# Attention A in 64-column matmuls with a new order of its batch, and one read moved in attention B

## What is computed

```python
# attention A: 16 heads of 8, R = 8 value groups, on a normalised x
xn = _ln(x, g1, b1)
q = _lin(xn, Wq, bq).reshape(b, n, H, HD) / np.sqrt(HD)
k = _lin(xn, Wk, bk).reshape(b, n, H, HD)
score = softmax(einsum('bihd,bjhd->bhij', q, k), axis=-1)
v = _lin(xn, Wv, bv).reshape(b, n, R, HD)
out = einsum('bhij,bjrd->bihrd', score, v)
comp = softmax(concatenate([qv, out], axis=-1) @ Ws.T + bs, axis=3)
out = (comp * out).sum(axis=3).reshape(b, n, DIM)
...
# the program
x = x + attn_a(_layernorm(x))      # attn_a: the above, then a dense block with its own norm
x = x + ffn(_layernorm(x))         # two matrices without an activation between: folded into one
x = x + attn_b(_layernorm(x))      # attention with a memory, segments of 64 tokens
x = x + ffn(_layernorm(x))
```

## Time and profile before

| | us |
|---|---|
| median of 3 runs | 1479.66 (1475.42 to 1479.83) |
| the profiled execution | 1480.59 |
| its span, first to last instruction | 1478.7 |

### The profile page before, as it was taken

How to read it: one execution, slowest core, us unless ns; L and a number is a source line. 1 busy time by engine, 2 the same in 40 slices (tenths; PEclk the granted TensorE clock), 3 DMA queues, 4 the chain that set the end, 5 groups by cost and what they waited for, 6 DMA issues and landing times. The chain is left out here.

```text
span 1478.7 us, 53395 instructions
## 1 busy us (share of the span) xinstructions
PE 1279.3 (87%) x17796; PEld 1160.4 (78%) x17796; DVE 1014.3 (69%) x2754; ACT 886.4 (60%) x2084; POOL 874.4 (59%) x1167
## 2 busy tenths in 40 slices
PE   5999999999999999999984877648989898888896
PEld 4799898998898999899973666427878778777785
DVE  3558778778778788788762444346777777777764
ACT  2456666666676676666652666445665656565653
POOL 3546676676676776667644888564444444444441
PEclk9899999999999999999995999869999999999998
DMA  5443332332332332322303444135454444454541
GB/s 145 122 130 95 83 107 64 95 99 71 96 89 80 97 89 81 96 78 79 97 8 114 122 129 128 43 106 140 144 141 136 145 137 147 137 147 138 147 137 42
DMA packets 181703, 158.26 MB, mean 107 GB/s; under 512 B 12529, under 2 KB 163185, under 8 KB 181618
## 3 DMA queue, kind: packets, MB, share of 16 engines
q1 hardware_dynamic: 181618, 157.17, 36.9%
HBM read 113.09 MB, written 44.04 MB: 106 GB/s over the span
## 5 line engine op out<-in xcount | busy, mean ns | idle before, releaser
L609 PE MATMUL a_bank<-a_vp,a_prob 128*128 128x74 f32 x4096 | 598.7, 253 | 0.0
L609 PEld LDWEIGHTS a_bank<-a_vp,a_prob 128*128 128x128 f32 x4096 | 588.6, 192 | 5.7 <-issue 0.3
L697 DVE TENSOR_REDUCE a_nmax<-a_bank 128x2 f32<-128x512 f32 x512 | 344.7, 684 | 155.3 <-PE a_bank L578 155.0
L496 ACT ACTIVATE a_prob<-a_bank 128x512 f32<-128x512 f32 x512 | 305.3, 596 | 211.4 <-PE a_bank L593 206.0
L578 PE MATMUL a_bank<-a_k_st,a_q_st 96*128 96x256 bf16 x1024 | 260.8, 278 | 35.5 <-DVE a_nmax L697 25.6
L593 PE MATMUL a_bank<-a_q_st,a_k_st 120*128 120x256 bf16 x1024 | 281.8, 276 | 1.8 <-POOL a_q_st L345 1.8
L1480 ACT ACTIVATE c_prob<-c_bank 128x256 f32<-128x256 f32 x256 | 98.7, 386 | 124.5 <-PE c_bank L1630 123.0
L416 POOL TENSOR_TENSOR a_prod<-a_ov,a_wgt 128x512 f32<-128x512 f32 x128 | 151.6, 1184 | 34.1 <-POOL a_prod L416 17.2
L345 POOL TENSOR_SCALAR a_q_st<-a_mt 24x2048 bf16<-24x2048 bf16 x64 | 121.4, 1896 | 83.5 <-ACT a_mt L470 43.3
L578 PEld LDWEIGHTS a_bank<-a_k_st,a_q_st 96*128 96x128 bf16 x1024 | 129.7, 134 | 47.9 <-DVE a_nmax L697 34.6
L593 PEld LDWEIGHTS a_bank<-a_q_st,a_k_st 120*128 120x128 bf16 x1024 | 140.3, 137 | 10.7 <-issue 2.2
(11 more groups left out here) (201 smaller groups left out, 2672.2 us busy)
## 6 DMA issues: line engine op xcount, KB each, us to landing
a_q_st<-scratch_a_parts_dram SPq DMA_DIRECT2D x64, 288.0 KB
a_k_st<-scratch_a_parts_dram SPq DMA_DIRECT2D x192, 96.0 KB
c_q_st<-scratch_c_parts_dram SPq DMA_DIRECT2D x64, 288.0 KB
c_k_st<-scratch_c_parts_dram SPq DMA_DIRECT2D x192, 96.0 KB
scratch_a_parts_dram<-a_parts SPq DMA_DIRECT2D x32, 384.0 KB, 2.7
scratch_c_parts_dram<-c_parts SPq DMA_DIRECT2D x32, 384.0 KB, 3.5
a_x<-in_x SPq DMA_DIRECT2D x32, 128.0 KB, 3.1
scratch_y<-a_y SPq DMA_DIRECT2D x32, 128.0 KB, 2.7
```

Of the source, the lines that this page charges most:

```text
L496: act.activation(prob[h % 4][:, :, :].rearrange("p a b -> p (a b)"), t_ps[h % 2][:, :], ACT.Exp).then_inc(exped, 1)
L609: mm = pe.matmul(o_ps[g % 2][:, at:at + VM], prob[h % 4][:, c, t * P:(t + 1) * P], vp[o][:, c, 0:VM], start=c == 0, stop=c == NT - 1)
L697: dve.tensor_reduce(nmax[:, t, 2 * g:2 * g + 2, 0], s_ps[t][:, :].rearrange("p (h k) -> p h k", h=2), AX.X, ALU.max, negate=True).then_inc ...
```

## The change

In attention A: all matmuls of scores, shifts, values, q, k and v are issued as two of 64 stationary columns (`columns`); the transposes keep their width. One unit of the first pass stands in every slot. The second pass starts at slot 15 in place of 13, and the transposes of the maxima move to slots 11 and 3. z is computed from x directly, with its own scale and shift: since var(y) = var(x) / (var(x) + eps), both norms come out of one power over (var + eps) and ((1 + eps) var + eps^2). z is made at slot 12, before y at slot 13, transposed at slot 14, xn at slot 15, all one body earlier; q and k stand at slot 0. POOL does splits 1 and 2, the spread of lag 2, splits 3 and 4, the weighing step, the norm, the spread of lag 1 and the products, in this order. DVE's order is new, and its sums are four of half a tile each. All loops are opened with a hint for their back edge. In attention B `read(2, 2, i)` stands ahead of the step on at_b.

```diff
+    with nc.Fori(PEELED // 2, end, engines=[eng.engine], hint_back_edge=True) as j:
...
-        SPLIT, NORM, MP, POST = 4, 8, 10, 9
-        OFF, PVLAG = 13, 2
-        S_AT = (0, 0, 1, 2, 2, 3, 4, 5, 6, 7, 8, 9, 10, 11, 12, 13)
-        MT_AT = (10, 2)
-        PIECES, STAGES, FOLDED = 4, 5, 8
+        SPLIT, NORM, MP, POST, SUMS = 4, 5, 10, 9, 4
+        OFF, PVLAG = 15, 2
+        MT_AT = (11, 3)
+        Z_AT, ZT_AT, XN_AT, QK_AT = 12, 14, 15, 0
+        PIECES, STAGES, FOLDED, COLS = 4, 5, 8, P // 2
...
                     if not isinstance(j, int) or n >= 0:
                         sp.wait_ge(y_d, (n + 1) * NT)
                         apart(sp, spare)
+                        sp.wait_ge(z_d, (n + 1) * NT)
+                        apart(sp, spare)
...
+                    norm(1, pool.tensor_scalar(rt[:, 0, :], mv[:, :, 1], EPS, None, ALU.add))
+                    norm(2, pool.tensor_scalar(negm[:, :], mv[:, :, 0], -1.0, None, ALU.mult))
+                    norm(3, pool.tensor_scalar(rt[:, 1, :], mv[:, :, 1], 1.0 + EPS, EPS * EPS, ALU.mult, ALU.add))
+                    norm(4, pool.tensor_tensor(rs[:, :, :], rt[:, :, :], half[:, :, :], ALU.pow))
+                    norm(5, pool.tensor_tensor(shift[:, :, :], negm[:, :].unsqueeze(1).broadcast_to([P, 2, NT]),
+                                               rs[:, :, :], ALU.mult))
...
+                    if s == QK_AT + 1 and active(j, u, 0):
+                        act.wait_ge(qk_p, n + 1)
...
+                    if s == Z_AT and active(j, u, -1):
...
+                            act.activation(z[1 - i][:, t, :], x[1 - i][:, t, :], ACT.Identity,
+                                           scale=rs[:, 1, t:t + 1], bias=shift[:, 1, t:t + 1]).then_inc(z_d, 1)
...
+                    if s == XN_AT and active(j, u, -1):
+                        act.wait_ge(z_t, n + 2)
+                        act.activation(xn[1 - i][:, :], zv_ps[:, 0:T], ACT.Identity, scale=cols[:, 2:3],
+                                       bias=cols[:, 3:4]).then_inc(xn_d, 1)
...
+                def columns(out, lhsT, rhs, start=True, stop=True):
+
+                    for a in range(P // COLS):
+                        cs = slice(a * COLS, (a + 1) * COLS)
+                        mm = pe.matmul(out[cs, :], lhsT[:, cs], rhs, start=start, stop=stop)
+                    return mm
...
-                    mm = pe.matmul(o_ps[g % 2][:, at:at + VM], prob[h % 4][:, c, t * P:(t + 1) * P],
-                                   vp[o][:, c, 0:VM], start=c == 0, stop=c == NT - 1)
+                    mm = columns(o_ps[g % 2][:, at:at + VM], prob[h % 4][:, c, t * P:(t + 1) * P],
+                                 vp[o][:, c, 0:VM], start=c == 0, stop=c == NT - 1)
...
+                    if s == QK_AT and active(j, u, 0):
                         pe.wait_ge(xn_d, n + 1)
                         if not isinstance(j, int) or n >= 2:
-                            pe.wait_ge(mt_d, 2 * (n - 1))
-                        pe.matmul(qk_ps[:, 0:T], w_q[:, :], xn[i][:, :], start=True, stop=True)
-                        pe.matmul(qk_ps[:, T:2 * T], w_k[:, :], xn[i][:, :], start=True, stop=True).then_inc(qk_p, 1)
+                            pe.wait_ge(mt_d, 2 * n - 3)
+                        columns(qk_ps[:, 0:T], w_q[:, :], xn[i][:, :])
+                        columns(qk_ps[:, T:2 * T], w_k[:, :], xn[i][:, :]).then_inc(qk_p, 1)
...
                         if k < NT and active(j, u, lag):
                             shift(n - lag, h, (i + lag) % 2, k)
-                        if k >= 2:
-                            for w, hh in halves[(k - 2) * len(units):(k - 1) * len(units)]:
-                                score_half(w, hh)
+                        if k >= 2 and active(j, u, 1):
+                            score_half(s, k - 2)
                         if active(j, u, plag):
                             values(n - plag, ph, (i + plag) % 2, k)
...
                 reduces(0, 1)
-                weighs(0, 2)
+                moments(0)
                 reduces(1, 2)
-                weighs(2, 4)
+                moments(1)
                 reduces(2, 3)
...
+                weighs(0, 1)
+                reduces(3, 4)
+                weighs(1, 2)
+                reduces(4, 5)
+                weighs(2, 3)
                 reduces(5, 6)
...
+                weighs(3, 4)
+                reduces(6, 7)
+                summed(0)
+                reduces(7, 8)
                 splits(0)
                 reduces(8, 9)
+                new_values()
+                reduces(9, 10)
                 weighs(5, 6)
-                reduces(9, 10)
+                reduces(10, 11)
                 weighs(6, 8)
-                reduces(10, 11)
+                reduces(11, 12)
                 weighs(8, POST)
...
                 reduces(12, 13)
...
+                summed(1)
+                reduces(13, 14)
+                summed(2)
+                reduces(14, 15)
+                summed(3)
+                reduces(15, H)
                 splits(1)
...
                 remember(2, 2)
+                read(2, 2, i)
                 if active(j, u, 3):
...
                     dve.scalar_tensor_tensor(at_b[:, SEG:T], ps_a[:, T + SEG:2 * T], beta[:, 2:3],
                                              at_b[:, SEG:T], ALU.mult, ALU.add).then_inc(at_d, 1)
-                read(2, 2, i)
                 reduce_unit(2)
```

More of the change, by code:

```diff
@@ L134, in attention_a @@
         mv = sb("a_mv", [P, NT, 2])
[L135 to L138, removed]
+        rt, rs, shift = (sb(f"a_{a}", [P, 2, NT]) for a in ("rt", "rs", "shift"))
+        negm = sb("a_negm", [P, NT])
         xn = [sb(f"a_xn{i}", [P, T]) for i in range(2)]
@@ L327, in _ @@
         def _(pool):
[L328 removed]
+            pool.memset(half[:, :, :], -0.5).then_inc(half_d, 1)
             pool.wait_ge(half_d, 1)
@@ L352, in body, with split, norm @@
                 i = u
+                def split(k, ins):
+                    ins.then_inc(split_d, 1)
+                    pool.wait_ge(split_d, n * SPLIT + k)
+                    apart(pool, spare)
+                def norm(k, ins):
+                    ins.then_inc(norm_d, 1)
+                    if k >= NORM - 2:
+                        pool.wait_ge(norm_d, (n + 1) * NORM + k)
+                        apart(pool, spare)
+                if active(j, u, 0):
+                    pool.wait_ge(qk_d, (n + 1) * 2)
+                    if not isinstance(j, int) or n >= 2:
+                        pool.wait_ge(parts_out, (n - 1) * 16)
+                    apart(pool, spare)
+                    split(1, pool.tensor_scalar(parts[i][:, :, 0, :], qk[i][:, :, :], 1.0, 0.0, ALU.mult, ALU.add))
+                    split(2, pool.tensor_tensor(rest[:, :, :], qk[i][:, :, :], parts[i][:, :, 0, :], ALU.subtract))
                 if active(j, u, 2):
                     spread(1, n - 2, i)
+                if active(j, u, 0):
+                    apart(pool, spare)
+                    split(3, pool.tensor_scalar(parts[i][:, :, 1, :], rest[:, :, :], 1.0, 0.0, ALU.mult, ALU.add))
+                    split(4, pool.tensor_tensor(parts[i][:, :, 2, :], rest[:, :, :], parts[i][:, :, 1, :],
+                                                ALU.subtract))
                 if active(j, u, 3):
@@ L363, in body @@
                     pool.wait_ge(post, b * POST + 5)
[L364 to L385, removed]
                 if active(j, u, -1):
@@ L577, in score_half @@
                             pe.wait_ge(maxed, b * H + w - 1)
-                    mm = pe.matmul(s_ps[t][:, hh * T:(hh + 1) * T],
-                                   q_st[o][0:MROW, 2 * g + hh, t * P:(t + 1) * P],
-                                   k_st[o][0:MROW, 2 * g + hh, :], start=True, stop=True)
+                    mm = columns(s_ps[t][:, hh * T:(hh + 1) * T],
+                                 q_st[o][0:MROW, 2 * g + hh, t * P:(t + 1) * P],
+                                 k_st[o][0:MROW, 2 * g + hh, :])
                     if hh:
@@ L592, in shift @@
                             pe.wait_ge(exped, b * H + h - 1)
-                    mm = pe.matmul(t_ps[h % 2][:, c * T:(c + 1) * T],
-                                   k_st[o][0:AROWS, h, c * P:(c + 1) * P], q_st[o][0:AROWS, h, :],
-                                   start=True, stop=True)
+                    mm = columns(t_ps[h % 2][:, c * T:(c + 1) * T],
+                                 k_st[o][0:AROWS, h, c * P:(c + 1) * P], q_st[o][0:AROWS, h, :])
                     if c:
@@ L656, in body @@
                     plag, ph = (lag, h - PVLAG) if h >= PVLAG else (lag + 1, h + H - PVLAG)
-                    units = [w for w in range(H) if S_AT[w] == s] if active(j, u, 1) else []
-                    halves = [(w, hh) for w in units for hh in range(2)]
                     for k in range(4):
@@ L719, in moments @@
                 def moments(k):
-                    t = k % NT
+                    if not active(j, u, -1):
```

(11 more changed lines are left out.)

142 lines of the change are left out of this document (56 added, 86 removed).

## The result

The changed kernel takes 1414.38 us (median of 4 runs, 1411.13 to 1418.39), against 1478.01 for the kernel before beside it; the ratio is 0.955 (0.952 to 0.958). The prediction was 1361: the sign and most steps held, but the gain is 64 us where 119 was forecast, and the time lies above the 1340 to 1385 that were given for it, near rival (b)'s 1409. The profiled execution took 1416.97 us.

What follows compares the result with a forecast made beforehand. Attention A was taken as bound by PE's stream, with a small bunching wait. Period 17.9 + 1.5 + 0.3 = 19.7 us against 22.44 saves 85, less 2 fill; with B's 36, 1480.6 - 83 - 36 gives 1361 us, range 1340 to 1385.

Steps and rivals of the forecast that it cites:

- rival (b): Attention A: larger waits for xn and DVE, or POOL's chain late for slot 15; period 21.2 us, 1409 us; chance 0.17.
- PE's step: Attention A: one bf16 plus one f32 matmul falls from 0.290 to 0.237 us with 64 stationary columns; bounds 0.23 and 0.29.
- the rival that the halves run one after the other: Attention A: column halves do not overlap where bf16 and f32 alternate; step 0.474 us, whole kernel 1833 us; chance 0.04.
- PE's work per batch: Attention A: PE's gapless work falls from 21.2 to 17.9 us per batch.
- The hole: Head of each attention A batch: PE waits for xn before q and k, 1.5 us; bounds 0 and 2.2.
- y's activations: Attention A, slot 13: y's two ACT activations push ACT back by another 0.3 us before xn.
- DVE's floor: Attention A: DVE needs 17.9 us busy, some 0.5 of handoffs and 0.1 for halved sums, 18.5 us per batch.
- The a_nmax term: Attention A: of DVE's reductions only unit 10 still holds PE, by about 0.3 us per batch.
- DVE uses the hole ... so its floor does not add to it: Attention A: during PE's wait for xn, DVE does unit 15 and the second splits; its 18.5 us adds nothing.
- The hint at nothing: Loop back edges: the hint was costed at 0 us, as PE's idle time left none for the back edges.
- B: Attention B: the earlier read shortens PE's wait before c_uv, 1.3 us in 28 batches, 36 us; bounds 0 and 44.6.
- the chain through DRAM: Attention B: parts and stacks must close in the shorter period; the gain per batch was lowered from 1.4 to 1.3 us.

Runs made afterwards that it cites:

- both: Changed kernel with DVE's two blocked weighing instructions moved ahead of POOL's spread and ACT's xn at the head of slot 15: 1337.92 us, ratio 0.906.
- xn_early: Changed kernel with only ACT's xn moved to the head of slot 15, ahead of the exponential and the a_ov copy: 1382.34 us, ratio 0.937.

## Why the prediction was right in its sign and short in its size

1. **PE's step: right.** 0.24 us against 0.237, and the rival that the halves run one after the other (1833) is out. The Trainium skill, TensorEngine Tiling (Array Packing), When to Use Tiling, gives column tiling for a stationary width of 64 or less. The trace does not bear that out as a limit: at a width of 128 the step fell from 0.29 to 0.24 us.
2. **PE's work per batch: mis-sized a little.** 17.9 was forecast. The change has 21.47 less its waits (34.3/12 = 2.86), 18.6; in both, with fewer stalls, 18.96 less 0.8 (10.8 us of waits in 258 us, 13.6 batches) is 18.2.
3. **The hole: right in mechanism, 0.98 us for 1.5.** I added whole durations of ACT's instructions. They overlap: the last exponential starts at 424.37, the copy at 424.87, xn at 425.15 and ends at 425.73, so 1.36 us for the 1.56 of the sum. And the 0.3 that was added for y's activations did not arise: ACT stands 0.45 us waiting for PE before this exponential, so it was not behind.

```profile
424.37 0.60 ACT L488 ACTIVATE a_prob<-a_bank 128x512 f32<-128x512 f32 x1 [0.45 <-PE a_bank L571]
424.87 0.40 ACT L497 COPY a_ov<-a_bank 128x292 f32<-128x292 f32 x1
425.15 0.58 ACT L522 ACTIVATE a_xn<-a_bank,a_cols 128x256 f32<-128x256 f32 x1
```

4. **DVE's floor: the step that failed.** "The change adds little: ... +0.1" took DVE's busy time over from the kernel before. The new orders put two instructions under POOL's spread, 2.8 us per batch over their free durations and 2.2 more than before's order lost, and DVE's busy time rose by 2.0 us to 19.9. The a_nmax term became 1.72 in place of 0.3. Of the period's excess of 1.77 us that is 1.4; PE's work has 0.7 more, the wait behind the loop 0.2, and the hole 0.5 less than forecast. Moving the two instructions gave back 1.61 us. Going through the slots, I used free durations, and did not lay POOL's order beside DVE's.
5. **"DVE uses the hole ... so its floor does not add to it": wrong.** xn_early showed it: closing the hole gave 0.89 us of its 0.98 with DVE at 94%.
6. **The hint at nothing: wrong.** It costs 8 to 9 us here and brings nothing to this order, though in before's order the columns need it (30 us). "How a loop with twice the PE instructions branches, no row shows" was said, and left without a bound.
7. **B: right.** 31.4 us for 36; read late again, 35 us back. The period is 422.6/31 = 13.63 for 13.3, and what the prediction took off for the chain through DRAM was too little, as SP's queue now has a part in it.

The period's parts: 0.98 (xn) + 1.72 (a_nmax) + 0.16 (issue) of waits were measured; the 18.6 that is left of the 21.47 counts as PE's work. The rival that gave a period of 21.2 and 1409 us was nearest in the number. Its larger DVE wait came, but its larger hole did not (0.98 us), and POOL's chain mattered by blocking DVE and not by being late; so the nearness is in part luck.

## What to carry to other kernels

When an order of work is changed by hand, lay the engines' timelines over each other and look for two-input DVE operations that meet a long GpSimd instruction: the price is the rest of that instruction. Moving two such operations by one or two places took 1.61 us off a period of 21.47 here, though a third then met part of it. Split a 128-column stationary in two where f32 matmuls of few moving columns alternate with bf16 ones, but expect the time only once the operands and the other engines can follow. Where two engines feed each other unit by unit, add up the waits; don't take the largest busy time as the floor.

## What the hardware showed that was not expected

- A DVE instruction of 0.19 us took 1.47, and one of 0.42 took 1.93, behind one GpSimd instruction of 1.90 us; DVE's reductions of scores were not held: in the kernel both, two of them start at 478.47 and last 1.33 us together, beside a spread from 478.67 to 480.57.
- A hardware loop of 812 matmuls per turn had a back edge of 0.21 us in one order and of 5.2 us in another, with about nine more fetches of 16 KB for each long branch; a hint at the back edge brought it to 0.22.
- The same hint cost 8 to 9 us where the branch was short anyway, with 1.9 and 2.9 us of it at PE behind the loop's end.
